# Cross attention of a decoder layer: context loaded turned, its norm moved into the key-value weights

## The chip, the cores and the metric

The kernel runs on one core of one Trainium2 chip. A core has TensorE (matrix products, results in PSUM), VectorE, ScalarE and GpSimd for work on elements, and a queue engine (SyncE, SP) that starts transfers between DRAM and on-chip memory (SBUF). Each engine works through its own list of instructions and waits on semaphores for the others. The metric is the device time of one execution in microseconds; lower is better.

## What is computed

A decoder layer on 32 sequences of 112 tokens, width 256: a mixer with a state-space scan and its MLP, cross attention with 16 heads over a context of 375 rows, and a feed-forward layer with 8-bit rounding. The change touches the context's side of cross attention and its preparation:

```python
def layer_norm(x, g, b):
    mu = jnp.mean(x, axis=-1, keepdims=True)
    var = jnp.var(x, axis=-1, keepdims=True)
    return (x - mu) * jax.lax.rsqrt(var + EPS) * g + b
...
kv = cn @ Wkv
k, v = jnp.split(kv, 2, axis=-1)
sim = jnp.einsum('bhid,bjd->bhij', q, k) + mask[:, None, :, :]
attn = jax.nn.softmax(sim, axis=-1)
out = jnp.einsum('bhij,bjd->bhid', attn, v)
```

Here `cn` is the layer norm of the context, with gain `cln_g` and bias `cln_b`; one key head and one value head of 64 columns serve all 16 query heads. All of it is float32.

## The kernel before

Eight groups of four sequences pass through two parts. The first 613 us belong to the **mixer** (`mixer`): for group i, tiles of the input projection, a chain of factors on VectorE and GpSimd (`softplus`, `factors`, `chain`, `right`), then `scan(i)`, which multiplies in 56-row blocks (line 375), masks the result on VectorE (`causal_part`, line 791) and multiplies again (`scan_out`, line 361). `hidden` and `down` are its MLP.

The rest is **attention** (`attention`), groups of 28 steps, seven steps per sequence. In step p TensorE computes the scores of two heads' rows (line 1393), VectorE adds the mask and finds the extreme (`highest`, line 1793), ScalarE takes the exponential (line 1666), VectorE divides one step later (`divide`, line 1802), TensorE turns the probabilities two steps later (line 1400), ScalarE copies them (line 1660), and every three or four steps TensorE multiplies them with the values (line 1416). The scores of a step wait until `highest` of the step before is done.

Between these, `schedule()` puts *pieces* at fixed places `AT[p, "X"]` and `AT[p, "Y"]`, and all engines walk the same table: gate and value tiles of the gated MLP (steps 10 to 17), output tiles (1 to 8), the way back (9), the feed-forward tiles `up` (20 to 23) and `down` (25), query tiles (27). The norms of tokens, results and final output are spread over steps 20 to 22, 10 to 12 and 25 to 27 on VectorE. Each piece's PSUM bank (`seat`) is handed on by semaphores (`vacant`, `filled`, `emptied`). `START` is the order of the pieces ahead of the first group, among the last tiles of the mixer's MLP (`("mlp", n)`).

The context of the next sequence takes this path. SyncE loads it with rows on partitions into one of two buffers `cx` (line 1303). In the first three steps of a sequence VectorE runs `context_norm`: statistics; the inverse root (ten small operations, `norm_root`, last one at line 77); the normalization in place (line 1143). In steps 3 and 4 TensorE does the piece `("turned", b, k)`, three transposes of 125x128 into PSUM (line 1500), and ScalarE copies each with the gain as scale and the bias (line 1711) into `cT`. In step 5 follows `("kv", b)`, the product of `cT` with the weights `wkv` (line 1507), in step 6 `("vback", b)`, which turns the values back (line 1513). ScalarE copies the keys twice, VectorE the values once.

Of the kernel before, what the change touches and what calls it, by code (L numbers as in the profile page):

```python
# [16 lines left out]
GB = 4  # L17
# [87 lines left out]
def mixer(nc, ctx0, PS, ident, i_in, x_dram, xm_dram, w):  # L105
# [136 lines left out]
    def sync(sp):  # L242
# [16 lines left out]
        tokens_in(2)  # L259
        for i in range(NG):  # L260
# [19 lines left out]
    def tensor(pe):  # L280
# [169 lines left out]
        pe.wait_ge(s_prep.sem, 1)  # L450
        for i in range(NG):
# [210 lines left out]
    def vector(dve):  # L662
# [210 lines left out]
        dve.wait_ge(s_w2.sem, 5 * 16)  # L873
        for i in range(NG):
# [156 lines left out]
CLN = 3 * JT + 1 + RSQRT  # L1031
# [5 lines left out]
def schedule():  # L1037
# [36 lines left out]
def seat(piece):  # L1074
# [5 lines left out]
    if piece[0] in ("turned", "kv", "vback"):  # L1080
        if piece[1] != 1:
            return 2
        return piece[2] if piece[0] == "turned" else int(piece[0] == "vback")
# [62 lines left out]
def attention(nc, ctx0, PS, apart, ident, xm_dram, ctx_dram, mask_dram, out_dram, w):  # L1146

    sb = Arena(nc, ARENA_AT)
    cx = sb("x_cx", [JP, 2, JT, D])
# [15 lines left out]
    cT = sb("x_cT", [128, KD, J])  # L1165
    kT = sb("x_kT", [128, 2, J])
# [38 lines left out]
    l_cx = [count(f"x_lcx{n}", 32) for n in range(2)]  # L1205
# [88 lines left out]

    def sync(sp, mlp):
# [6 lines left out]
        def contexts(i, b):  # L1302
            sp.dma_start(cx[:, b % 2, :, :], ctx_dram[i * GB + b, :, :].rearrange("(t p) d -> p t d", p=JP)).then_inc(l_cx[b % 2].sem, 16)
# [4 lines left out]
        def group(it, first=False, last=False):  # L1308
            for p in range(STEPS):
# [18 lines left out]
                if p == 6:  # L1328
                    filled(sp, it, ("turned", 1, 1))
                    contexts(it, 3)  # L1330
                if p == 13 and not last:
                    filled(sp, it, ("turned", 2, 1))
                    contexts(it + 1, 0)
                if p == 20 and not last:
                    filled(sp, it, ("turned", 3, 1))
                    contexts(it + 1, 1)
                if p == 26 and not last:
                    filled(sp, it, ("turned", 0, 1))
                    contexts(it + 1, 2)
# [10 lines left out]
        sp.dma_start(cols[:, :], w["x_cols"]).then_inc(l_q.sem, 16)  # L1350
        contexts(0, 0)
        contexts(0, 1)
        scanned()
        sp.dma_start(wq[:, :, :], w["x_wq"]).then_inc(l_q.sem, 16)
        sp.dma_start(wkv[:, :, :], w["x_wkv"]).then_inc(l_kv.sem, 16)
# [26 lines left out]
    def tensor(pe, mlp):  # L1382
# [235 lines left out]
        for piece in START:  # L1618
# [3 lines left out]
            if piece == ("turned", 0, 0):  # L1622
                result_taken(LAST - 1)
# [462 lines left out]
```

## Time and profile before

| | us |
|---|---|
| median of three runs | 1927.63 |
| lowest and highest | 1926.17, 1927.75 |
| the profiled execution | 1927.04 |
| its span, first to last instruction | 1925.2 |

| engine | busy, us | share of the span |
|---|---|---|
| TensorE, matmuls | 1819.9 | 95% |
| TensorE, weight loads (overlap) | 1075.7 | 56% |
| VectorE | 1286.4 | 67% |
| ScalarE | 954.6 | 50% |
| GpSimd | 420.2 | 22% |

The DMA queue of SyncE occupies 15.1% of the transfer engines' time. The granted clock of TensorE was 0.982 of full speed in the mean. Busy shares are means over stages with different limits; a busy TensorE says nothing of how its matmuls overlap. The chain that ended last tells on which engine the end hung, and the rows in order of time tell what stands where.

### The profile page before, as it was taken

To read this page: it belongs to the slowest core of one execution; us is meant where nothing else is said; L and a number is where in the kernel's file an instruction comes from. 1 tells how busy PE (TensorE), PEld (TensorE's weight loads), DVE (VectorE), ACT (ScalarE), POOL (GpSimd) and SP (SyncE) were. 2 spreads that over 40 slices of the span, in tenths; PEclk is the share of its full clock that TensorE was granted. 3 is DMA by queue.
4 is the path that set the end of the run, shared out by engine and by line. 5 is a ranking of instruction groups with operands and counts; after the bars stand their busy time and mean duration, and the time that the engine had idled before them with its cause. 6 is when DMAs were issued, how large, how long until landed. Compare 5 with 4: busy or idle time off the path is not lost.

```text
span 1925.2 us, 28637 instructions
## 1 busy us (share of the span) xinstructions
PE 1819.9 (95%) x9696; PEld 1075.7 (56%) x9696; DVE 1286.4 (67%) x3998; ACT 954.6 (50%) x2326; POOL 420.2 (22%) x569
## 2 busy tenths in 40 slices
PE   4589999999999998999999999999999999999997
PEld 2456766766767544455455555555545555555566
DVE  6688888888867487376567557557747655764743
ACT  3343553553441456456455545545645654654542
POOL 4777876876871000000000000000000000000000
PEclk8689999999999999999999999999999999999998
DMA  4000000000013232111121112112111111111100
GB/s 124 1 1 11 11 10 11 20 11 14 8 36 125 56 126 61 37 54 50 45 59 48 50 50 57 46 45 54 53 50 50 49 50 55 48 50 45 37 16 20
DMA packets 63538, 84.01 MB, mean 44 GB/s; under 512 B 5121, under 2 KB 62113, under 8 KB 62497
## 3 DMA queue, kind: packets, MB, share of 16 engines
q1 hardware_dynamic: 62928, 81.72, 15.1%
q8 instruction: 79, 1.29, 0.3%
q14 instruction: 67, 0.54, 0.1%
q10 hardware_dynamic: 464, 0.46, 0.1%
HBM read 74.82 MB, written 7.34 MB: 43 GB/s over the span
## 4 chain that ended last, share of the span: by engine, by line
PE 89%; DVE 7%; ACT 2%; issue 1%; DMA 0%; DVEq 0%; ACTq 0%
PE ps L1438 19%; PE ps L1393 9%; PE ps L1431 9%; PE ps L1400 9%; PE ps L1416 8%; PE ps L292 7%; PE ps L429 5%; PE ps L411 4%; PE ps L375 4%; PE ps L391 3%; PE ps L1507 2%; PE ps L1547 1%; PE ps L1492 1%; PE ps L361 1%; PE ps L1500 1%
## 5 line engine op out<-in xcount | busy, mean ns | idle before, releaser
L1793 DVE CUSTOM_DVE_ANT_0 x_pr<-ps,x_mk 128x375 f32<-128x375 f32 x448 | 228.0, 546 | 322.5 <-issue 204.2
L1660 ACT ACTIVATE x_pT<-ps 125x384 f32<-125x384 f32 x448 | 195.6, 490 | 252.6 <-PE ps L1400 251.8
L1666 ACT ACTIVATE x_pr<-x_pr,x_mx 128x375 f32<-128x375 f32 x448 | 268.3, 608 | 38.2 <-DVE x_mx L1793 38.1
L1400 PEld LDWEIGHTS ps<-ident,x_pr 128*125 128x125 f32 x1344 | 163.8, 187 | 129.6 <-issue 96.8
L1393 PE MATMUL ps<-x_kT,x_qT 64*128 64x375 f32 x896 | 202.5, 527 | 23.3 <-DVE x_mx L1793 17.3
L1400 PE MATMUL ps<-ident,x_pr 128*125 128x128 f32 x1344 | 206.1, 290 | 0.1
L1438 PE MATMUL ps<-x_xn,x_w 128*128 128x448 f32 x512 | 203.9, 541 | 0.0
L1802 DVE TENSOR_SCALAR x_pr<-x_pr,x_rc 128x375 f32<-128x375 f32 x448 | 169.6, 421 | 8.0
L1416 PE MATMUL ps<-x_pT,x_va 125*64 125x512 f32 (+1 forms) x768 | 159.9, 552 | 0.6 <-ACT x_pT L1660 0.6
L292 PE MATMUL ps<-m_xa,w_in 128*128 128x448 f32 x352 | 145.3, 560 | 6.2 <-ACT m_xa L522 6.2
L1393 PEld LDWEIGHTS ps<-x_kT,x_qT 64*128 64x128 f32 x896 | 68.2, 184 | 143.7 <-issue 115.8
L1438 PEld LDWEIGHTS ps<-x_xn,x_w 128*128 128x128 f32 x512 | 92.8, 190 | 74.2 <-issue 71.4
L1676 ACT ACTIVATE x_OT<-ps 128x512 f32<-128x512 f32 x64 | 34.8, 544 | 188.3 <-PE ps L1416 188.3
L429 PE MATMUL ps<-fc,m_gl 128*112 128x256 f32 x512 | 113.3, 379 | 0.1
L1416 PEld LDWEIGHTS ps<-x_pT,x_va 125*64 125x64 f32 x768 | 49.7, 137 | 94.3 <-issue 93.4
L292 PEld LDWEIGHTS ps<-m_xa,w_in 128*128 128x128 f32 x352 | 66.9, 196 | 62.6 <-issue 55.7
L429 PEld LDWEIGHTS ps<-fc,m_gl 128*112 128x112 f32 x512 | 89.4, 177 | 19.6 <-issue 0.5
L1438 PE MATMUL ps<-x_xn,x_wq 128*128 128x448 f32 x256 | 99.2, 542 | 0.0
L1438 PE MATMUL ps<-f_xn,f_w 128*128 128x448 f32 x224 | 89.5, 543 | 0.0
L1431 PE MATMUL ps<-x_ff,x_w 128*128 128x448 f32 x224 | 89.5, 542 | 0.0
L1666 ACT ACTIVATION_READ_ACCUMULATOR x_pr<-x_pr,x_mx 128x1 f32 x448 | 89.3, 199 | 0.0
L1431 PE MATMUL ps<-x_OT,x_wo 128*128 128x448 f32 x224 | 88.9, 539 | 0.0
(194 smaller groups left out, 2999.1 us busy)
## 6 DMA issues: line engine op xcount, KB each, us to landing
x_mk<-in_mask SPq DMA_DIRECT2D x224, 187.5 KB, 2.4
x_cx<-in_context SPq DMA_DIRECT2D x32, 375.0 KB
x_mixed<-m_x SPq DMA_DIRECT2D x8, 448.0 KB, 3.4
X<-x_mixed SPq DMA_DIRECT2D x8, 448.0 KB, 4.5
m_X<-in_x SPq DMA_DIRECT2D x7, 448.0 KB, 4.0
out<-f_so SPq DMA_DIRECT2D x7, 448.0 KB, 3.4
fc<-in_fc SPq DMA_DIRECT2D x2, 1024.0 KB, 13.1
x_w<-in_x_w SPq DMA_DIRECT2D x1, 2048.0 KB, 8.3
```

Source lines behind the costliest of these rows:

```text
L292: last = pe.matmul(to, w_in[:, k, n * 128:(n + 1) * 128], xa[:, k, :], start=(k == 0), stop=(k == KD - 1))
L375: last = pe.matmul(bank(2 * (b % 2) + g)[0:rows, at], Rb[part, c, b, j * S:j * S + rows], Lm[part, c, b * NQ + j, :, :], start=(c == 0), s ...
L429: last = pe.matmul(bank(4 + b // 2 if i < LAST else 4)[0:S, (b % 2) * D:(b % 2 + 1) * D], gl[:, k, b * S:(b + 1) * S], fc2[:, k, :], start ...
L1393: pe.matmul(bank(e)[:, 0:J], qT[rows, b, r * ROWS:(r + 1) * ROWS], kT[rows, b % 2, :], start=True, stop=True).then_inc(h_s.sem, 1)
L1400: last = pe.transpose(bank(2 + e)[0:JP, t * ROWS:(t + 1) * ROWS], pr[:, 2 * (p % SLOT) + e, t * JP:(t + 1) * JP], ident[:, :])
L1416: last = pe.matmul(bank(4)[DH * e:DH * e + DH, 0:n * ROWS], va[:, b % 2, t, :], pT[:, k + e:k + 2 * n:2, t, :], start=(t == 0), stop=(t == ...
L1431: last = pe.matmul(to[:, 0:T], lhs, rhs, start=(m == 0), stop=(m == KA + KH - 1))
L1438: last = pe.matmul(to[:, 0:T], weights[:, k, at:at + 128], moving[:, k, :], start=(k == 0), stop=(k == KD - 1))
L1660: act.activation(pT[:, 2 * NV * (batch(p) % 2) + 2 * (p % NP % NV) + e, :, :].rearrange("p t s -> p (t s)"), bank(2 + e)[0:JP, 0:JT * ROWS ...
L1666: act.activation(pr[:, k, :], pr[:, k, :], ACT.Exp, scale=-1.0, bias=mx[:, k:k + 1], accum_out=sums[:, k:k + 1]).then_inc(h_e.sem, 1)
L1793: dve.tensor_tensor_reduce(pr[:, k + e, :], bank(e)[:, 0:J], mk[:, p % SLOT, :], -1.0, 3.0e38, ALU.add, ALU.min, mx[:, k + e:k + e + 1]).t ...
L1802: dve.tensor_scalar(pr[:, k + e, :], pr[:, k + e, :], rc[:, k + e:k + e + 1], None, ALU.mult).then_inc(h_n.sem, 1)
```

## The change

The context is given to the kernel a second time, transposed, and loaded directly as `cT`. The copy with rows on partitions is still loaded, into one buffer, for the statistics alone. The layer norm is taken apart. Gain and mean go into the weights once: `centred` multiplies row d of `wkv` by the gain and subtracts, for each column, the mean over the rows of gain times weight, so that the product with the raw context already has its mean removed. The bias times the weights becomes a column `kvb`, added when keys and values leave PSUM. The inverse root of each context row must scale a column of `cT`: the 375 roots are written to DRAM (`roots_out`), read back onto all 128 partitions as `rb` (`roots_in`), and VectorE multiplies `cT` by it (two products of 128x375, `context_norm` stage 2). This stage moves from the third to the fifth step of a sequence (`CONTEXT = (0, 1, 4)`). The pieces `turned` with their transposes and ScalarE copies are gone; `kv` and `vback` keep their steps. In `START` the first `kv` and `vback` stand later.

```diff
@@ mixer, tensor @@
         pe.wait_ge(s_prep.sem, 1)
+        pe.wait_ge(a_dB.sem, a_dB.value(0, 2))
+        column_means(pe)
         for i in range(NG):
             scan(i)
@@ mixer, vector @@
         dve.wait_ge(s_w2.sem, 5 * 16)
+        centred(dve)
         for i in range(NG):
@@ schedule @@
-    for b, places in ((1, ((3, "X"), (4, "X"), (5, "X"), (6, "X"))), (2, ((10, "X"), (11, "X"), (12, "X"), (13, "X"))),
-                      (3, ((17, "X"), (18, "X"), (19, "X"), (20, "X"))), (0, ((24, "X"), (25, "X"), (26, "X"), (27, "X")))):
-        for place, piece in zip(places, (("turned", b, 0), ("turned", b, 1), ("kv", b), ("vback", b))):
-            at[place].insert(0, piece)
+    for b in range(GB):
+        for r, kind in ((NP - 2, "kv"), (NP - 1, "vback")):
+            at[(b - 1) % GB * NP + r, "X"].insert(0, (kind, b))
@@ attention @@
+    def early_loads(sp):
+        sp.dma_start(cols[:, :], w["x_cols"]).then_inc(l_kv.sem, 16)
+        sp.dma_start(wkv[:, :, :], w["x_wkv"]).then_inc(l_kv.sem, 16)
+
+    def column_means(pe):
+        pe.wait_ge(w_col.sem, 1)
+        for k in range(KD):
+            pe.matmul(bank(4)[:, 0:2 * DH], cgm[:, k:k + 1].to_broadcast([128, 128]), wkv[:, k, :], start=(k == 0), stop=(k == KD - 1))
+        for k in range(KD):
+            last = pe.matmul(bank(4)[:, 2 * DH:2 * DH + 1], wkv[:, k, :], cb[:, k:k + 1], start=(k == 0), stop=(k == KD - 1))
+        last.then_inc(w_mean.sem, 1)
+        pe.wait_ge(w_done.sem, KD + 1)
+
+    def centred(dve):
+        dve.wait_ge(l_kv.sem, 2 * 16)
+        dve.tensor_scalar(cgm[:, :], cg, 1.0 / D, None, ALU.mult).then_inc(w_col.sem, 1)
+        dve.wait_ge(w_mean.sem, 1)
+        for k in range(KD):
+            dve.scalar_tensor_tensor(out=wkv[:, k, :], in0=wkv[:, k, :], scalar=cg[:, k:k + 1], in1=bank(4)[:, 0:2 * DH],
+                                     op0=ALU.mult, op1=ALU.subtract).then_inc(w_done.sem, 1)
+        dve.tensor_copy(kvb[:, :], bank(4)[:, 2 * DH:2 * DH + 1]).then_inc(w_done.sem, 1)
@@ attention, sync @@
+        def turned_in(i, b):
+            sp.dma_start(cT[:, :, :], ctx_turned[i * GB + b, :, :].rearrange("(k p) j -> p k j", p=128)).then_inc(l_ct.sem, 16)
+
+        def roots_out(i, b):
+            sp.wait_ge(c_ln.sem, c_ln.value(i, CLN * b + CROOT))
+            sp.dma_start(roots_dram[:, :], st[0:JP, 16 + JT:16 + 2 * JT]).then_inc(l_rs.sem, 16)
+
+        def roots_in(i, b):
+            sp.wait_ge(l_rs.sem, l_rs.value(i, 16 * (b + 1)))
+            sp.dma_start(rb[:, :], roots_dram[:, :].rearrange("p t -> (p t)").unsqueeze(0).to_broadcast([128, J])).then_inc(l_rb.sem, 16)
...
+                if r == 1:
+                    filled(sp, made_in(it, b), ("kv", b))
+                    turned_in(g, n)
+                if r == 2:
+                    roots_out(g, n)
+                    if g + (n + 1) // GB < NG:
+                        contexts(g + (n + 1) // GB, (n + 1) % GB)
+                if r == 3:
+                    roots_in(g, n)
...
         sp.dma_start(w1[:, :, :], w["x_w1"]).then_inc(l_w1.sem, 16)
+        roots_out(0, 0)
+        contexts(0, 1)
+        roots_in(0, 0)
@@ attention, tensor @@
-            elif kind == "turned":
...
-                for t in range(JT):
-                    last = pe.transpose(to[:, t * JP:(t + 1) * JP], cx[:, b % 2, t, n * 128:(n + 1) * 128], ident[0:JP, 0:JP])
-                last.then_inc(done, 1)
             elif kind == "kv":
-                for k in range(KD):
-                    emptied(pe, it, ("turned", n, k))
+                pe.wait_ge(c_ln.sem, c_ln.value(held_by(it, n), CLN * (n + 1)))
@@ attention, scalar @@
-                act.activation(cT[:, n, :], src[:, 0:J], ACT.Identity, scale=cg[:, n:n + 1], bias=cb[:, n:n + 1]).then_inc(done, 1)
...
-                act.activation(kT[0:DH, n % 2, :], src[0:DH, 0:J], ACT.Copy)
+                act.activation(kT[0:DH, n % 2, :], src[0:DH, 0:J], ACT.Identity, bias=kvb[0:DH, :])
@@ attention, vector @@
-                norm_apply(dve, lambda t: cx[:, c, t, :], lambda t: cx[:, c, t, :], c_mv[0:JP], c_st[0:JP], c_ln, JT)
+                dve.wait_ge(l_ct.sem, l_ct.value(i, 16 * (b + 1)))
+                dve.wait_ge(l_rb.sem, l_rb.value(i, 16 * (b + 1)))
+                for k in range(KD):
+                    dve.tensor_tensor(cT[:, k, :], cT[:, k, :], rb[:, :], ALU.mult).then_inc(c_ln.sem, 1)
```

TensorE's list ahead of the first scan, before (`m_xa` is the mixer's normed input, `m_Lm` and `m_R` the scan's factors; the first 56 rows are block 0):

```order
L292 MATMUL ps<-m_xa,w_in 128x448 [waits a_xn,a_abs]
L292 MATMUL ps<-m_xa,w_in 128x448
L375 MATMUL ps<-m_Lm,m_R 16x64 [waits a_Lm,a_uTc,a_R,m_prep,m_w2]
L375 MATMUL ps<-m_Lm,m_R 16x64 x3
L375 MATMUL ps<-m_Lm,m_R 32x64 x4
```

And in the changed kernel (`x_wkv` are the key-value weights, `x_cgm` the gain over 256):

```order
L293 MATMUL ps<-m_xa,w_in 128x448 [waits a_xn,a_abs]
L293 MATMUL ps<-m_xa,w_in 128x448
L1314 MATMUL ps<-x_wkv,x_cgm 128x128 [waits a_dB,w_col,m_prep,m_w2]
L1314 MATMUL ps<-x_wkv,x_cgm 128x128
L1316 MATMUL ps<-x_cols,x_wkv 128x1 x2
L376 MATMUL ps<-m_Lm,m_R 16x64 [waits a_Lm,a_R,a_uTc,w_done]
L376 MATMUL ps<-m_Lm,m_R 16x64 x3
```

The scan now waits for `w_done`, which VectorE raises; VectorE's list has the counterpart behind the cast of the causal mask:

```order
L874 CAST causal<-m_gl 112x448 [waits m_caus]
L1322 TENSOR_SCALAR x_cgm<-x_cols 128x2 [waits x_lkv,m_w2,m_zero]
L1325 SCALAR_TENSOR_TENSOR x_wkv<-x_wkv,x_cols,ps 128x128 [waits w_mean]
L1325 SCALAR_TENSOR_TENSOR x_wkv<-x_wkv,x_cols,ps 128x128
L1327 COPY x_kvb<-ps 128x1
L794 COPY_PREDICATED m_MT<-causal,ps 112x448 [waits b_mt] x4
```

Four instructions stand there ahead of the first masked copy, which used to follow the cast.

TensorE's list in step 18 of a group and into step 19, before (`x_pr` probabilities, `x_cx` context, `f_x` tokens of the feed-forward layer):

```order
L1400 MATMUL ps<-ident,x_pr 125x128 [waits h_c,h_n]
L1400 MATMUL ps<-ident,x_pr 125x128 x2
L1500 MATMUL ps<-ident,x_cx 128x125 [waits x_free2]
L1500 MATMUL ps<-ident,x_cx 128x125 x2
L1445 MATMUL ps<-ident,f_x_127 128x112 [waits x_free0,o_ln]
L1445 MATMUL ps<-ident,f_x_127 128x112 x3
```

And in the changed kernel:

```order
L1445 MATMUL ps<-ident,x_pr 125x128 [waits h_c,h_n]
L1445 MATMUL ps<-ident,x_pr 125x128 x2
L1490 MATMUL ps<-ident,f_x_130 128x112 [waits x_free0,o_ln]
L1490 MATMUL ps<-ident,f_x_130 128x112 x3
```

The three transposes are gone and the next piece follows directly; the same holds at the seven other places of a group.

VectorE's list in step 25 of a group, before (`x_th` holds the rounded sum, `f_so` the final tokens):

```order
L1799 RECIPROCAL x_rc<-x_sum 128x2 [waits h_e]
L1802 TENSOR_SCALAR x_pr<-x_pr,x_rc 128x375 [waits h_r]
L1802 TENSOR_SCALAR x_pr<-x_pr,x_rc 128x375
L1874 TENSOR_TENSOR x_th<-ps,f_b2q 112x512 [waits x_full0]
L1878 TENSOR_TENSOR f_so<-x_th,f_x_127 112x512 [waits f_out,x_free0]
```

And in the changed kernel:

```order
L1828 RECIPROCAL x_rc<-x_sum 128x2 [waits h_e]
L1831 TENSOR_SCALAR x_pr<-x_pr,x_rc 128x375 [waits h_r]
L1831 TENSOR_SCALAR x_pr<-x_pr,x_rc 128x375
L1844 TENSOR_TENSOR x_cT<-x_cT,x_rb 128x375 [waits x_lrb,x_lct]
L1844 TENSOR_TENSOR x_cT<-x_cT,x_rb 128x375
L1906 TENSOR_TENSOR x_th<-ps,f_b2q 112x512 [waits x_full0]
L1910 TENSOR_TENSOR f_so<-x_th,f_x_130 112x512 [waits f_out,x_free0]
```

The two products with the spread roots stand in front of the evacuation of the `down` product, with the waits for the two transfers.

## Rows read from the trace of the kernel before

**Rows 1.** The page, the chain that ended last, by engine.

```profile
PE 89%; DVE 7%; ACT 2%; issue 1%; DMA 0%; DVEq 0%; ACTq 0%
```

**Rows 2.** Groups by line: names, shapes, count | busy us, mean ns | idle before.

```profile
L1711 ACT ACTIVATE x_cT<-ps,x_cols 128x375 f32<-128x375 f32 x64 | 42.3, 660 | 0.0
...
L1143 DVE TENSOR_SCALAR x_cx<-x_cx,x_mv,x_st 125x256 f32<-125x256 f32 x96 | 33.7, 407 | 0.0
...
L1500 PE MATMUL ps<-ident,x_cx 125*128 125x125 f32 x192 | 31.2, 270 | 0.1
```

**Rows 3.** TensorE in order of time, a steady group: start us, duration us, instructions.

```profile
1030.63 0.48 PE L1500 MATMUL ps<-ident,x_cx 125*128 125x125 f32 x3
1030.95 3.17 PE L1438 MATMUL ps<-x_xn,x_w 128*128 128x448 f32 x8
...
1068.37 0.48 PE L1500 MATMUL ps<-ident,x_cx 125*128 125x125 f32 x3
1068.83 3.67 PE L1492 MATMUL ps<-f_w2q,f_hq 128*112 128x256 fp8e4 x32
```

**Rows 4.** The same view, step 27; in brackets the idle time before, and its releaser.

```profile
1076.54 0.90 PE L1393 MATMUL ps<-x_kT,x_qT 64*128 64x375 f32 x4 [1.09 <-DVE x_mx L1793]
```

**Rows 5.** VectorE in order of time, steps 22 and 25 of the same group.

```profile
1057.83 0.16 DVE L77 SCALAR_TENSOR_TENSOR x_st<-x_st 125x3 f32<-125x3 f32 x1
...
1068.95 0.74 DVE L1802 TENSOR_SCALAR x_pr<-x_pr,x_rc 128x375 f32<-128x375 f32 x2
1070.80 0.69 DVE L1874 TENSOR_TENSOR x_th<-ps,f_b2q 112x512 f16<-112x512 f32 x1 [1.10 <-PE ps L1492]
```

**Rows 6.** VectorE in order of time, a float32 product out of SBUF.

```profile
83.74 0.62 DVE L748 TENSOR_TENSOR m_D<-m_rs,m_L 128x448 f32<-128x448 f32 x1
```

**Rows 7.** TensorE in order of time, the first scan.

```profile
78.43 7.67 PE L375 MATMUL ps<-m_Lm,m_R 64*16 64x64 f32 x112 [3.13 <-POOL m_R L987]
91.72 1.76 PE L361 MATMUL ps<-m_MT,m_uT 112*64 112x112 f32 x16 [5.63 <-DVE m_MT L791]
...
96.97 0.99 PE L361 MATMUL ps<-m_MT,m_uT 112*64 112x112 f32 x16
97.89 2.38 PE L375 MATMUL ps<-m_Lm,m_R 64*16 64x64 f32 x56
```

**Rows 8.** VectorE in order of time, the same stretch.

```profile
90.04 0.39 DVE L871 CAST causal<-m_gl 112x448 int8<-112x448 f32 x1
...
93.53 1.05 DVE L799 SCALAR_TENSOR_TENSOR m_u<-m_u,cols,ps 128x112 f32<-128x112 f32 x4 [0.78 <-PE ps L361]
```

**Rows 9.** TensorE in order of time, products with one moving column.

```profile
115.57 1.64 PE L319 MATMUL ps<-cols,m_r 128*112 128x1 f32 x16
```

**Rows 10.** Stretches: bounds us, length, TensorE busy (count), granted clock, DMA share, GB/s.

```profile
95.00:96.00 1.00, 1.00 (x20) 0.50 0.00 0
...
97.00:98.00 1.00, 1.00 (x22) 1.00 0.00 0
```

**Rows 11.** The page, transfers: issues, KB each, median us to landing.

```profile
x_mk<-in_mask SPq DMA_DIRECT2D x224, 187.5 KB, 2.4
...
x_w<-in_x_w SPq DMA_DIRECT2D x1, 2048.0 KB, 8.3
```

**Rows 12.** Stretches, all engines: a microsecond in which only contexts are loaded.

```profile
559.00:560.00 1.00, 1.00 (x7) 0.81 (x6) 0.96 (x3) 0.91 (x2) 1.00 (x1) 1.00 0.34 121
```

**Rows 13.** The opening of attention in order of time: SyncE, VectorE, TensorE.

```profile
613.51 0.35 SPq L1363 DMA_DIRECT2D x_w<-in_x_w  x1
...
614.86 0.16 DVE L77 SCALAR_TENSOR_TENSOR x_st<-x_st 125x3 f32<-125x3 f32 x1
...
614.66 3.27 PE L481 MATMUL ps<-m_xb,fc 128*128 128x448 f32 x8 [0.48 <-ACT m_xb L593]
...
619.28 1.67 PE L481 MATMUL ps<-m_xb,fc 128*128 128x448 f32 x4
620.78 1.67 PE L1438 MATMUL ps<-x_xn,x_wq 128*128 128x448 f32 x4
```

More of the change, by code:

```diff
@@ L659, in scalar, with vector @@
         return gelu
-    def vector(dve):
+    def vector(dve, centred):
         def roots(i):
@@ L1030 @@
 RESULT, TOKENS, FINAL = (10, 11, 12), (20, 21, 22), (25, 26, 27)
-CLN = 3 * JT + 1 + RSQRT
+CONTEXT = (0, 1, 4)
+CROOT = 2 * JT + 1 + RSQRT
+CLN = CROOT + KD
 GH = GB // 2
@@ L1079, in seat @@
         return 2
[L1080 to L1083, printed above, removed]
+    if piece[0] in ("kv", "vback"):
+        return 2 if piece[1] != 1 else int(piece[0] == "vback")
     return piece[-1] % 2
@@ L1204, in attention @@
     s_q = count("f_q", 0)
-    l_cx = [count(f"x_lcx{n}", 32) for n in range(2)]
+    l_cx = count("x_lcx", 16 * GB)
+    l_ct = count("x_lct", 16 * GB)
+    l_rs = count("x_lrs", 16 * GB)
+    l_rb = count("x_lrb", 16 * GB)
+    w_col = count("w_col", 0)
+    w_mean = count("w_mean", 0)
+    w_done = count("w_done", 0)
     l_mk = [count(f"x_lmk{n}", 16 * STEPS // SLOT) for n in range(SLOT)]
@@ L1327, in group @@
                         sp.dma_start(dst, src).then_inc(l_up.sem, 16)
[L1328 to L1339, printed above, removed]
+                b, r = divmod(p, NP)
+                if last and b == GB - 1:
+                    continue
+                n, g = (b + 1) % GB, it + (b + 1) // GB
+                if r == 1:
[7 more added lines that the diff above has]
+                    roots_in(g, n)
             if not first:
@@ L1621, in tensor @@
                 continue
-            if piece == ("turned", 0, 0):
+            if piece == ("kv", 0):
                 result_taken(LAST - 1)
-            if piece == ("kv", 0):
-                pe.wait_ge(l_kv.sem, 16)
             part(-1, piece)
@@ L1705, in part @@
                 act.activation(hq[:, n, :], src[:, 0:T], ACT.Relu, bias=fb1[:, n:n + 1], saturate=False).then_inc(done, 1)
-            elif kind == "turned":
-                b = piece[1]
-                src, done = filled(act, it, piece)
-                if n == 0 and it >= 0:
-                    filled(act, it if b != 1 else it - 1, ("kv", (b - 1) % GB))
-                act.activation(cT[:, n, :], src[:, 0:J], ACT.Identity, scale=cg[:, n:n + 1], bias=cb[:, n:n + 1]).then_inc(done, 1)
             elif kind == "kv":
@@ L1919, in group @@
                 b, r = divmod(p, NP)
-                if r < 3 and not (last and b == GB - 1):
-                    context_norm(it, (b + 1) % GB, r)
+                if r in CONTEXT and not (last and b == GB - 1):
+                    context_norm(it, (b + 1) % GB, CONTEXT.index(r))
                 if p in TOKENS and not last:
@@ L1987, in program @@
         mix = mixer(nc, ctx, PS, ident, i_in, x, xm, w)
-        att = attention(nc, ctx, PS, apart, ident, xm, ctx_dram, mask_dram, out, w)
+        att = attention(nc, ctx, PS, apart, ident, xm, ctx_dram, ctx_turned, roots, mask_dram, out, w)
         block = ctx.enter_context(nc.Block())
@@ L2079 @@
     x = given("x", np.asarray(inputs["x"]))
-    context = given("context", np.asarray(inputs["ctx_1024"]))
+    context = np.asarray(inputs["ctx_1024"])
+    turned = given("context_turned", context.transpose(0, 2, 1))
+    context = given("context", context)
     mask = np.asarray(inputs["mask_BxSxS2_ff0"])
@@ L2083 @@
     out = nc.dram_tensor("out", (B, S, D), FP32, kind="ExternalOutput").ap()
-    program(nc, x, context, mask, w, out)
+    program(nc, x, context, turned, mask, w, out)
     return run_bass_kernel_spmd(nc, [arrays], core_ids=[0]).results[0]["out"]
```

61 lines of the change are left out of this document (30 added, 31 removed).

## The prediction

> **What bounds the kernel now.** I read the chain that ended last first. TensorE holds 89% of it, VectorE 7% [rows 1]. So work taken from TensorE is time, wherever TensorE has no wait behind it; work taken from ScalarE or VectorE alone is not. Then I read the rows by line for the three parts of the old path: 192 context transposes on TensorE, 64 ScalarE copies that also apply scale and bias, 96 VectorE normalizations [rows 2]. Then TensorE's order of time in a steady group of attention: rows follow each other without a gap, the context pieces among them [rows 3]. The exception in such a group is one wait of 1.09 us on VectorE [rows 4]. Last I read the start, where the change puts new work ahead of the first scan, and the transfers.
>
> **What one context piece is worth.** The row by line says 31.2 us busy for 192 transposes, 0.27 us each [rows 2], but they overlap, so busy time is the wrong price. The right one is the shift of the next row: a piece of three starts at 1030.63 and the next matmul at 1030.95, that is 0.32 us; the piece ahead of the 8-bit matmuls starts at 1068.37 and they start at 1068.83, 0.46 us [rows 3]. There are 64 pieces (32 contexts by two). Six of them, at step 25 of groups 1 to 6, have the 8-bit product behind them: 6 x 0.46 = 2.8 us. The other 58 x 0.325 = 18.8 us. Together **21.6 us** if every piece lies on the path.
>
> Do they? Two places need a look. At steps 24 and 25 TensorE would come 0.33 + 0.46 = 0.79 us earlier to the down product, and the VectorE scaling of the turned context now sits in step 25 in front of that product's evacuation. Before, VectorE finished its division at 1069.69 and then waited 1.10 us for TensorE until 1070.80 [rows 5]. The nearest row for the new operation is the float32 SBUF product of 448 columns, 0.62 us [rows 6]; two of 375 columns take 2 x 0.62 x 375/448 = 1.04 us, 1.1 with their overhead. So VectorE, 0.33 us earlier after the shorter step 24, is free at about 1070.4, and TensorE's product is ready at 1070.0. The 0.4 us lost there sits ahead of a second wait for TensorE and is gone by step 26. The scores' wait of 1.09 us [rows 4] moves along as a whole. A quarter of the saving could be lost here, not more.
>
> By the Trainium skill, "VectorE: DVE Perf Modes", the TRN2 errata section, a float32 tensor_tensor takes (N + 151)/0.96 ns, an estimate of 0.55 us for 375 columns and 1.1 us for two. For 448 columns the formula gives 0.62 us, and the trace agrees with 0.62 us [rows 6]; by it the sum would not change.
>
> The other place is steps 17 to 19, with little TensorE work in two of them. ScalarE loses two copies of 0.66 us there [rows 2], more than TensorE loses, and VectorE's three normalizations (3 x 0.41 = 1.2 us of rows, 1.05 overlapped) are replaced by 1.1 us. Neither engine gets more work, so I keep the whole saving. In group 0 VectorE is late in several steps and some of the 8 pieces (2.6 us) may be lost; I leave them in, because the old wait on the ScalarE copy of the context vanishes as well. Bounds of the gain: 21.6 + 1.5 = 23 above; 21.6 less group 0 (2.6) less the pieces of steps 24 and 25 (6 x 0.79 = 4.7) = 14.3 below.
>
> **The prologue.** The weights are now centred between the first tiles and the first scan: VectorE scales a column, TensorE multiplies, VectorE corrects the weights, and TensorE waits for it. This looks like nothing, four small matmuls. But TensorE did the first two blocks of the scan, 112 rows of matmuls from 78.43 us on, while VectorE was still busy until 90.43 with the next group's factors, and stood ready at 91.72 [rows 7, 8]. Those blocks were hidden. Now they stand behind VectorE's first free moment. Step by step: the cast ends at 90.43 [rows 8]; the column scale is a tiny operation of 0.16 us [rows 5]: 90.65. TensorE's four matmuls are 8 rows; a row of one column with 128 loaded rows takes 1.64/16 = 0.10 us at the full clock [rows 9], 0.2 at half, and the granted clock is half there, 0.50, that is 1.2 GHz [rows 10]: 1.7 us, 92.4. VectorE's two corrections cost 1.05/4 = 0.26 us each [rows 8], the bias copy 0.17: 93.1. The first block is half of 7.67 us [rows 7]: 97.0. I take the clock as full from there, as it was from 97 us on before [rows 10]; the second block is 2.38 us [rows 7]: 99.3. The first product with the weights of the scan starts there instead of at 91.72. It catches up a little, since it and the next block run at the full clock (0.99 and 2.38 overlapped, 3.3 us, where they took 96.97 - 91.72 = 5.25): 102.6 against 96.97, **5.6 us late**. From there TensorE and, in the second group, a VectorE chain fed by it run on with no slack that is not behind this point, so all of it reaches the end. Bounds: everything at full clock (92.3 + 2.4 + 2.4 + 3.3 = 100.2) costs 3.2 us; everything at half clock (93.1 + 7.7 + 5.25 = 106.1) costs 9.1 us.
>
> **The roots' round trip.** Roots go to DRAM in 125 rows of 12 bytes and come back as one row spread over 128 partitions. The trace has no such transfer. The nearest are a mask of 187.5 KB at 2.4 us and, for what can lie ahead in the queue, a context at 0.34 of the engines and 121 GB/s (384 KB, 3.2 us) [rows 11, 12]. Two in series with one context ahead: 2 x 2.4 + 3.2 = 8.0 us. The shortest time available is at the end of a group: the roots are ready at 1057.99 and VectorE wants the spread row at 1069.69 - 0.33 = 1069.4 [rows 5], 11.4 us. Everywhere else it is more, so I cost it at nothing; below that there is no gain. In the opening, roots are ready at 615.02 [rows 13], behind 2 MB of weights that land after 8.3 us [rows 11] (issued at 613.51 [rows 13], so 621.8), then 2.4, then 3.2 + 2.4: 629.8, and two products: 630.9. The first key-value product is now behind 12 tiles of 1.50 us from 614.66 on [rows 13], at 632.7. It fits with 1.8 us to spare; were it late, that is paid once. Turned contexts add 12.3 MB to a queue that is mostly idle and have three steps to land: nothing. The key-value copies get a bias, on ScalarE and VectorE, off the path: nothing.
>
> **Sum.** 21.6 - 5.6 = 16.0 us. The profiled execution took 1927.04 us (span 1925.2); the median of the runs shown is 1927.63, so the median after is 1927.63 - 16.0 = **1911.6 us**.
>
> **Rivals.**
> - *The prologue costs nothing* (VectorE or GpSimd decides the second group anyway): 1927.63 - 21.6 = 1906 us. Against it: all of VectorE's work in that stretch starts from TensorE's results. 12%.
> - *The short steps are bound elsewhere.* VectorE and ScalarE carry steps 17 to 19 and 24 to 27, and the scaling moved into steps 11 and 25, beside the two other norms, becomes what ends last: gain 14.3, less 5.6: 1918.9 us. For it: the 1.09 us wait [rows 4]. 18%.
> - *Slower: the round trip lands late.* It decides from 11.4 us on, at step 25 of groups 0 to 6, and VectorE's wait there holds the next scores. Each microsecond beyond costs 7; the gain is gone at 11.4 + 16.0/7 = 13.7 us. At 15 us it costs 25: 1937 us. Against it: 8.0 us from rows. 6%. The Trainium skill, "DMA: Bandwidth & Descriptors", speaks against the change here: its specifications say that pieces under 512 bytes are read, modified and written. No row here shows such a write. Its section on the anatomy of one DMA gives 2.0 us fixed, an estimate of 4.0 us for two, and by that nothing is late.
> - *Slower: the transposes were not on the path*, TensorE waiting as much as it saves: only the prologue stays, 1933 us. The gapless rows [rows 3] speak against it. 4%.
> - The forecast: 60%.
>
> **Range.** 1906 takes in the first rival and the upper gain (23 less 3.2 is 1907.8); 1922 takes in the lower gain with a dearer prologue (14.3 - 9.1 = 5.2 is 1922.4). About 0.2% (3.9 us) is what a measurement of this kernel can tell from no change: faster by more 0.89, within it 0.03, slower by more 0.08.
>
> **What would show it.** No context transposes; a matmul of the next piece right behind the probability transposes in steps 3, 4, 10, 11, 17, 18, 24 and 25; a steady group shorter by 2.7 us. The first product of the scan starts at about 99 us, and everything in the second group is 5 to 6 us late. VectorE's products on the context wait for no transfer. I am wrong if the groups shrink by less than 2 us, if VectorE waits for the spread roots, or if the lateness of the start fades by the fourth group.

## The result, and the profile after

The changed kernel takes **1915.5 us** (median of 4 runs, 1913.4 to 1916.9) against 1927.7 us for the kernel before (4 runs, 1926.2 to 1928.2) on the same chip: a ratio of 0.9941, 95% interval 0.9929 to 0.9952. In a later set of runs it was 1915.0 against 1927.2, 0.9933 (0.9917 to 0.9949). The gain is 12.2 us where 16.0 were forecast. The direction was right and the time lies inside the range; one term of the sum was too small by 3.8 us.

| | before | after |
|---|---|---|
| span of the profiled execution, us | 1925.2 | 1911.6 |
| VectorE's CAST, where the new prologue begins, us | 90.04 | 88.33 |
| TensorE's first token transposes of attention, us | 613.25 | 620.99 |
| from there to the end of the span, us | 1311.95 | 1290.6 |
| steady group of attention, us | 157.2 | 154.7 |

The two halves of the sum can be read apart. Attention is 21.3 us shorter; everything ahead of it is 7.7 us longer, and that in spite of an early part that ran 1.7 us faster by chance (VectorE's CAST, the conversion of the causal mask, comes 1.7 us sooner; TensorE's token transposes at 70 us fell in a stretch at half clock before, 1.70 us, and not after, 0.93). Profiles of one code differ by as much: in a second one of the changed kernel the CAST comes at 89.19 us, and in a version below that is the same up to there (the one with a longer round trip) at 90.04. From the CAST to the first token of attention it is 523.2 us before and 532.7 after (532.6 in the second profile): the prologue costs 9.5 us.

The chain that ended last, from the page of the changed kernel, answers [rows 1]; TensorE holds a little more of it:

```profile
PE 90%; DVE 6%; ACT 1%; issue 1%; DMA 1%; SPq 0%; DVEq 0%; ACTq 0%
```

TensorE's order of time in the changed kernel (start us, duration us, instructions, in brackets the idle time before and its releaser), the first scan, answers [rows 7]:

```profile
89.07 1.20 PE L1314 MATMUL ps<-x_wkv,x_cgm 128*128 128x128 f32 x4 [15.49 <-DVE x_cgm L1322]
90.06 0.85 PE L1316 MATMUL ps<-x_cols,x_wkv 128*128 128x1 f32 x4
91.68 8.27 PE L376 MATMUL ps<-m_Lm,m_R 64*16 64x64 f32 x112 [0.77 <-DVE x_kvb L1327]
99.88 1.76 PE L362 MATMUL ps<-m_MT,m_uT 112*64 112x112 f32 x16
101.57 3.23 PE L376 MATMUL ps<-m_Lm,m_R 64*16 64x64 f32 x56
104.72 0.99 PE L362 MATMUL ps<-m_MT,m_uT 112*64 112x112 f32 x16
```

VectorE in the same stretch, answers [rows 8]:

```profile
88.33 0.39 DVE L874 CAST causal<-m_gl 112x448 int8<-112x448 f32 x1
88.75 0.18 DVE L1322 TENSOR_SCALAR x_cgm<-x_cols 128x2 f32<-128x2 f32 x1
90.95 0.60 DVE L1325 SCALAR_TENSOR_TENSOR x_wkv<-x_wkv,x_cols,ps 128x128 f32<-128x128 f32 x2 [2.02 <-PE ps L1316]
91.47 0.15 DVE L1327 COPY x_kvb<-ps 128x1 f32<-128x1 f32 x1
```

The stretches of [rows 10] (bounds, length, TensorE busy, granted clock, DMA share, GB/s), now:

```profile
96.00:97.00 1.00, 1.00 (x22) 0.50 0.00 0
102.00:103.00 1.00, 1.00 (x22) 0.50 0.00 0
103.00:104.00 1.00, 1.00 (x24) 0.75 0.00 0
104.00:105.00 1.00, 1.00 (x24) 1.00 0.00 0
```

TensorE had stood idle for 15.49 us. The clock was at half (1.2 GHz) when it began again at 89.07 us and stayed there until 103 us, through the means, the two scan blocks and the first products behind them. All six profiles in which the prologue stands here show this: the clock is back 14 to 15 us after TensorE begins again. The 112 products of the two blocks take 8.27 us, all of it now on the path.

In attention the pieces are gone and the rows close up. TensorE around steps 24 to 27 of a steady group, the place of [rows 3, 4]:

```profile
1065.90 0.92 PE L1445 MATMUL ps<-ident,x_pr 128*125 128x128 f32 x6
1066.88 3.67 PE L1537 MATMUL ps<-f_w2q,f_hq 128*112 128x256 fp8e4 x32
...
1072.07 1.43 PE L1543 MATMUL ps<-x_cT,x_wkv 128*128 128x375 f32 x4
1074.58 0.90 PE L1438 MATMUL ps<-x_kT,x_qT 64*128 64x375 f32 x4 [1.08 <-DVE x_mx L1822]
```

The scores' wait for VectorE is 1.08 us, as it was (1.09). And the group's length, from its first query product to the next group's (the same row of before stood at 1081.41 and 1238.59):

```profile
1079.46 1.77 PE L1483 MATMUL ps<-x_xn,x_wq 128*128 128x448 f32 x4
...
1234.14 2.15 PE L1483 MATMUL ps<-x_xn,x_wq 128*128 128x448 f32 x5
```

154.7 us against 157.2: 2.5 us a group, where the text forecast 2.7.

The roots' way at the end of the same kind of group (SyncE's queue and VectorE): written at 1056.62, read back from 1059.67, needed at 1067.88, no wait.

```profile
1056.62 0.28 SPq L1344 DMA_DIRECT2D context_roots<-x_st  x1
1056.94 0.34 SPq L1337 DMA_DIRECT2D x_cx<-in_context  x1
1058.97 0.35 SPq L1334 DMA_DIRECT2D x_mk<-in_mask  x1
1059.67 0.35 SPq L1348 DMA_DIRECT2D x_rb<-context_roots  x1
...
1067.88 1.00 DVE L1844 TENSOR_TENSOR x_cT<-x_cT,x_rb 128x375 f32<-128x375 f32 x2
```

The row by line of the scaling shows all its waits for a transfer in the whole kernel, 6.4 us in two places: 5.4 us in the opening, under which TensorE goes on, and 1.0 us at the end of the first group.

```profile
L1844 DVE TENSOR_TENSOR x_cT<-x_cT,x_rb 128x375 f32<-128x375 f32 x64 | 32.1, 543 | 6.4 <-DMA x_rb<-context_roots 6.4
```

### The profile page after: what moved, and what is told of

Read it like the earlier page. It is cut to its first block, busy times and chain, and to the rows that moved or that the text cites. A ratio compares the mean times of both kernels' runs of the same rounds, so it can differ in the third digit from the quotient of the medians.

```text
span 1911.6 us, 28245 instructions
## 1 busy us (share of the span) xinstructions
PE 1800.1 (94%) x9512; PEld 1056.6 (55%) x9512; DVE 1285.3 (67%) x3970; ACT 925.4 (48%) x2262; POOL 418.2 (22%) x569
## 4 chain that ended last, share of the span: by engine, by line
PE 90%; DVE 6%; ACT 1%; issue 1%; DMA 1%; SPq 0%; DVEq 0%; ACTq 0%
PE ps L1483 20%; PE ps L1438 9%; PE ps L1445 9%; PE ps L1476 9%; PE ps L1461 8%; PE ps L293 7%; PE ps L430 6%; PE ps L412 4%; PE ps L376 4%; PE ps L392 3%; PE ps L1543 2%; PE ps L1583 1%; PE ps L1537 1%; PE ps L362 1%; PE ps L1549 1%
## 5 line engine op out<-in xcount | busy, mean ns | idle before, releaser
L1438 PE MATMUL ps<-x_kT,x_qT 64*128 64x375 f32 x896 | 202.5, 527 | 23.7 <-DVE x_mx L1822 17.7
L430 PE MATMUL ps<-fc,m_gl 128*112 128x256 f32 x512 | 113.2, 379 | 0.0
L430 PEld LDWEIGHTS ps<-fc,m_gl 128*112 128x112 f32 x512 | 89.4, 177 | 19.3 <-issue 0.5
## 6 DMA issues: line engine op xcount, KB each, us to landing
x_mk<-in_mask SPq DMA_DIRECT2D x224, 187.5 KB, 2.4
x_rb<-context_roots SPq DMA_DIRECT2D x32, 187.5 KB, 5.2
```

The source lines that it names most:

```text
L430: last = pe.matmul(bank(4 + b // 2 if i < LAST else 4)[0:S, (b % 2) * D:(b % 2 + 1) * D], gl[:, k, b * S:(b + 1) * S], fc2[:, k, :], start ...
L1438: pe.matmul(bank(e)[:, 0:J], qT[rows, b, r * ROWS:(r + 1) * ROWS], kT[rows, b % 2, :], start=True, stop=True).then_inc(h_s.sem, 1)
```

## Experiments

Two theories stood at the start. **A**: the prologue costs 9.5 us, because the two scan blocks have lost their cover and because TensorE, woken at half clock, stays there. **B**: the prologue costs the 5.6 us of the prediction, and the rest of the shortfall lies in attention. The comparisons name the kernel before; each set of runs had its own runs of it, all between 1925.9 and 1927.2 us in the median. A difference between two kernels of different sets is uncertain by as much as these differ, 1 to 2 us.

### The means behind the two blocks

```diff
-        column_means(pe)
         for i in range(NG):
             scan(i)
...
+                if i == 0 and b == 1:
+                    column_means(pe)
                 if b >= 1:
                     scan_out(b - 1)
```

> TensorE computes the column means after the scan's first two blocks of the first group (L376, 112 products) and ahead of the first scan_out, no longer ahead of the blocks; VectorE's part stays behind the CAST. Theory A (order): the changed kernel's prologue costs some 9.5 us, and most of it is that the 8.27 us of the two blocks, which before ran beside VectorE's softplus chain (78.43 to 86.1 us), now run behind the centring. Then the blocks go back beside the softplus, and what stays on the path is VectorE's L1322, the means on TensorE (2.0 us) and VectorE's L1325 and L1327 (0.75 us), some 3 us together, of which the clock may take a part: 1915.5 - 9.5 + 3 = 1909, the first MT product at about 93 to 94 us after the CAST's time of 88.3 and the second group's anchor (L293, 177.98) near 171.5. Theory B (the prologue costs the 5.6 us of the prediction, of which 1.6 were the blocks behind their wait, and the rest of the shortfall lies in attention): 1915.5 - 2.6 = 1913.

Measured: 1907.9 us (1907.3 to 1908.0), ratio to before 0.9900 (0.9885 to 0.9915). TensorE's rows:

```profile
78.70 7.33 PE L376 MATMUL ps<-m_Lm,m_R 64*16 64x64 f32 x112 [3.72 <-POOL m_R L992]
90.37 1.22 PE L1315 MATMUL ps<-x_wkv,x_cgm 128*128 128x128 f32 x4 [4.35 <-DVE x_cgm L1323]
91.39 0.85 PE L1317 MATMUL ps<-x_cols,x_wkv 128*128 128x1 f32 x4
94.16 1.76 PE L362 MATMUL ps<-m_MT,m_uT 112*64 112x112 f32 x16 [1.92 <-issue]
```

The blocks are back beside VectorE's softplus chain, and one moved call gives back 7.6 us. B allowed 2.6. It falls here.

### All of the prologue where the engines are idle

```diff
         rest_of_tiles(0)
+        pe.wait_ge(a_dB.sem, a_dB.value(0, 2))
+        column_means(pe)
         turn_u(0)
...
-        pe.wait_ge(a_dB.sem, a_dB.value(0, 2))
-        column_means(pe)
+        means_taken(pe)
         for i in range(NG):
             scan(i)
...
+            if i == 0:
+                mean_column(dve)
             scale_bc(i)
...
         tiles(0)
+        centred(dve)
         softplus(1)
...
         dve.wait_ge(s_w2.sem, 5 * 16)
-        centred(dve)
```

`mean_column` is the first operation of the old `centred`, `means_taken` the last wait of the old `column_means`.

> The same work in the idle time that both engines have earlier: VectorE's L1322 ahead of its wait for the first group's spread roots (3.58 us at L771), TensorE's means ahead of turn_u of group 0 (idle 11.6 us there), VectorE's L1325 and L1327 behind the first group's u (idle 8.67 us there). Theory A: the whole 9.5 us come back: 1906.0, with L346 to L293 of group 0 as in the kernel before and the first attention token at about 613.3 us instead of 620.99. Theory B: 5.6 us come back: 1909.9, with the first attention token near 615.4 us. If the new place collides with something (its bank, the clock), the token comes later than that.

Measured: 1904.9 us (1903.7 to 1906.4), ratio 0.9885 (0.9871 to 0.9900). TensorE, and behind it VectorE:

```profile
54.48 0.61 PE L1321 MATMUL ps<-x_wkv,x_cgm 128*128 128x128 f32 x4
54.92 0.51 PE L1323 MATMUL ps<-x_cols,x_wkv 128*128 128x1 f32 x4
66.97 3.74 PE L348 MATMUL ps<-ident,m_u 128*112 128x128 f32 x16 [11.54 <-DVE m_u L726]
```

```profile
66.84 0.59 DVE L1336 SCALAR_TENSOR_TENSOR x_wkv<-x_wkv,x_cols,ps 128x128 f32<-128x128 f32 x2
67.36 0.14 DVE L1338 COPY x_kvb<-ps 128x1 f32<-128x1 f32 x1
77.94 0.62 DVE L748 TENSOR_SCALAR m_rs<-ps 128x448 f32<-128x448 f32 x1 [10.44 <-ACT ps L540]
```

The same eight matmul rows take 1.0 us here, at the full clock, where they took 1.8 behind the 15 us of idleness, and both engines still wait behind them for others. This kernel, with the prologue in the idle time, was run once more beside the changed kernel, for a difference that rests on one set of runs:

> The changed kernel as it is, beside the two versions below on the same chip, so that their differences rest on the same runs: 1915.5.

> The kernel of hidden_prologue again. 10.6 us under the changed kernel if the prologue's price of the first runs holds (1904.9 against 1915.5, from different calls); 5.6 us under it by the prediction's term.

Measured: 1915.0 (1914.5 to 1915.8) and 1904.35 us (1903.9 to 1905.0), ratios to before 0.9933 (0.9917 to 0.9949) and 0.9877 (0.9861 to 0.9893). The difference is 10.6 us. In the profiles, from the transposes of the first u (L346 there, L348 here) to attention's first token, it is 554.5 against 544.7 us: 9.8.

### No prologue at all

```diff
-        column_means(pe)
...
-        centred(dve)
+    def centred(dve):
+        dve.memset(kvb[:, :], 0.0).then_inc(w_done.sem, 1)
```

> Leaves out the column means and the centring (the key-value weights are used as loaded, the bias is zero), all else as in the changed kernel. It prices the prologue by what is gained without it. Theory A: 9.5 us, 1906.0. Theory B: 5.6 us, 1909.9. Beside hidden_prologue it tells what the hidden work still costs (theory A: nothing).

Measured: 1904.5 us (1904.0 to 1906.8), ratio 0.9885 (0.9871 to 0.9900), the same as with the prologue hidden (1904.9). So the work itself costs nothing in its new place, and its old place cost all of some 10 us.

### The clock kept up

```diff
+        for _ in range(17):
+            pe.matmul(bank(4)[:, 0:T], w_in[:, 0, 0:128], xa[:, 0, :], start=True, stop=True)
         column_means(pe)
```

> The changed kernel with 17 more products of 128x448 on TensorE (their result is overwritten) in its idle 15.5 us ahead of the column means, to keep the granted clock at 1.00 until then. If the half clock is a part of the prologue's cost, the means take about 1 us instead of 2.05, the 112 products of the two blocks about 4.8 us (112 at the 42 ns of the 56 that took 2.38) instead of 8.27, the first scan_out 0.99 instead of 1.76 and the third block 2.38 instead of 3.23, together 6 us: 1909.5. If the clock plays no part (only the order): 1915.5.

Measured: 1909.7 us (1906.8 to 1911.5), ratio 0.9905 (0.9889 to 0.9922). TensorE's rows, one of VectorE's, and a stretch of four microseconds:

```profile
77.65 14.71 PE L454 MATMUL ps<-m_xa,w_in 128*128 128x448 f32 x34 [2.79 <-issue]
92.20 0.61 PE L1316 MATMUL ps<-x_wkv,x_cgm 128*128 128x128 f32 x4
...
93.92 4.69 PE L376 MATMUL ps<-m_Lm,m_R 64*16 64x64 f32 x112 [0.77 <-DVE x_kvb L1329]
98.53 0.99 PE L362 MATMUL ps<-m_MT,m_uT 112*64 112x112 f32 x16
99.45 2.38 PE L376 MATMUL ps<-m_Lm,m_R 64*16 64x64 f32 x56
```

```profile
90.02 0.18 DVE L1324 TENSOR_SCALAR x_cgm<-x_cols 128x2 f32<-128x2 f32 x1
```

```profile
88.00:92.00 4.00, 4.00 (x12) 1.00 0.00 0
```

Nothing was moved, 14.7 us of useless products were added, and the kernel is 5.8 us faster. The two blocks take 4.69 us instead of 8.27, the first product 0.99 instead of 1.76, the next block 2.38 instead of 3.23. Together with the means (1.72 us instead of 2.61 from their start to that of the blocks) these rows are 6.1 us shorter. Of the 4.8 us that still lie between this and the version with no cost (1909.7 against 1904.9), 1.9 belong to the useless products themselves: the column that the means wait for is ready at 90.20, in the changed kernel the means start 0.14 us behind it, and here they start at 92.20, when the last of these products is done. So of the prologue's 10 us, 6 to 7 are the half clock, and the order alone, at full clock, costs some 3. The Trainium skill, "TensorE: Matmul & The Clock Gate", Part 1, says that the throttled state is the default and activity releases it; the trace agrees with its two levels, 0.50 and 1.00, and in the changed kernel the release came only after 14 us of work.

The two cures don't add up:

> hidden_prologue with 11 more products of 128x448 on TensorE, three in its gap between dt_tile of group 1 and the first scan blocks, eight between these blocks and the first scan_out; their result is overwritten. If they keep the granted clock at 1.00 from 70 us on, the 112 products take 4.7 us instead of 7.7 (which buys nothing, VectorE is later), the first scan_out 0.99 instead of 1.76 and the second block 2.4 instead of 3.2: 1.6 us, 1903.3. If the clock falls all the same, the eight products take 1.7 us each and the first scan_out comes up to 7 us late: up to 1910.

Measured: 1904.65 us (1904.1 to 1906.7), ratio 0.9880 (0.9863 to 0.9896), no different from 1904.35 without. The clock did what it should from 80 us on (1.00, with the blocks at 4.69 us, first product 0.99, next block 2.38), and from the CAST to attention's first token the kernel took 520.6 us instead of 522.6. But in this execution all from 66 to 78 us ran at half clock, the projection tile in it (4 products from 72.38 us on) took 3.32 us instead of 1.74, and VectorE's CAST came later. The early clock differs like that between executions of one kernel: the same tile took 3.15 us in the first profile of the idle-time version and 1.74 in the second. That is worth as much as the 2 us.

### TensorE's transposes put back

```diff
                 to, done = vacant(pe, it, piece)
+                for k in range(KD):
+                    for t in range(JT):
+                        pe.transpose(to[:, t * JP:(t + 1) * JP], ident[0:JP, :], ident[0:JP, 0:JP])
                 for k in range(KD):
                     last = pe.matmul(to[:, 0:J], wkv[:, k, :], cT[:, k, :], start=(k == 0), stop=(k == KD - 1))
```

> The changed kernel with TensorE's 6 transposes of each context put back (of the unit matrix, into the bank that the key-value product then overwrites), nothing else of the old way. If the gain in attention is TensorE's time alone, as the prediction has it (64 pieces, 21.6 us with the two of the opening, 0.325 us a steady piece), nearly all of it goes: 1915.5 + 64 x 0.325 = 1936.3. If the short steps are bound elsewhere (the prediction's 14.3 us case): 1930. If ScalarE's L1711 copies or its wait were what the steps waited for: under 1925.

Measured: 1931.7 us (1930.1 to 1932.9), ratio 1.0030 (1.0019 to 1.0042): 16.2 us slower than the changed kernel, 17 to 19 if each is set against its own runs of the kernel before; either way less than the 20.8 expected. The six transposes of a context stand together ahead of its key-value product, not in the two steps of the old kernel. The steady group grows by 1.9 us, from 154.7 to 156.6. TensorE at the end of a group shows where the rest went:

```profile
1082.31 0.81 PE L1544 MATMUL ps<-ident 125*128 125x125 f32 x6
1082.95 1.43 PE L1546 MATMUL ps<-x_cT,x_wkv 128*128 128x375 f32 x4
1084.83 0.90 PE L1438 MATMUL ps<-x_kT,x_qT 64*128 64x375 f32 x4 [0.44 <-DVE x_mx L1825]
```

The scores behind them wait 0.44 us for VectorE where they waited 1.08: two pieces of 0.32 us run in a wait that was there. The other six of a group cost 0.32 us each. The opening and first group grow by 5.2 us for ten pieces, but 1.7 of this is a fall of the clock that this profile has and the changed kernel's doesn't: the 16 products of L430 from 654.27 us on take 5.39 us at a granted clock of 0.59 and 0.55, where they take 3.71 there. The ten pieces cost 3.5 us. And the last stretch lacks a fall of the clock that cost the changed kernel's profile 1.7 us (below). So the gain is TensorE's time, as forecast, and a piece costs its 0.32 us where TensorE doesn't wait right behind it.

### The round trip left out

The roots are neither written nor read; VectorE multiplies by ones, so the rows of the context are not scaled.

> Leaves out the round trip: the roots aren't written or read back, VectorE multiplies the turned context by a row of ones that is set once. The multiplications stay where they are. If the round trip costs nothing but the two waits that the trace shows (5.42 us of VectorE's time in the opening, under which TensorE goes on, and 0.96 us in the first group, where TensorE waits 0.9 us for the key-value product's operand): 1915.5 - 0.9 = 1914.6 at most. If the 32 small reads and writes disturb more (SyncE's queue, the masks behind them): 1912 or less.

Measured: 1912.5 us (1910.7 to 1913.8), ratio 0.9932 (0.9917 to 0.9947), 2.5 to 3 us under the changed kernel, whose runs begin at 1913.4. Set against the kernel before, the ratio is no different from the changed kernel's 0.9941 and 0.9933, so the medians don't separate the two. The profiles differ by 3.0 us. Group boundaries place it: 1.0 us in the first group, 0.3 in the seventh, and 1.7 in one place near the end, where the same 16 products of L1583 take 4.88 us in the changed kernel and 3.19 here. That is the clock. The changed kernel, then the one without the round trip:

```profile
1864.00:1865.00 1.00, 1.00 (x7) 0.89 0.51 150
1865.00:1866.00 1.00, 1.00 (x4) 0.50 0.91 278
```

```profile
1863.00:1864.00 1.00, 1.00 (x8) 1.00 0.85 249
1864.00:1865.00 1.00, 1.00 (x7) 1.00 0.66 209
```

The kernel before has that fall too, at 1878 us (4.87 us for its 16 products), and of the two profiles of the idle-time version one has it and one hasn't, so I don't count it as the round trip's. Nor the 0.3 us of the seventh group: in the version without a prologue, which has the round trip, that group takes 154.75 us against 154.70 here and 155.03 in the changed kernel. What is left is 1.0 us, of which 0.9 is the one wait of TensorE. I had expected 0.9.

### The round trip made longer

One copy of the roots from DRAM to DRAM, or three, between the write and the read:

```diff
+            for n in range(1):
+                sp.wait_ge(l_rs.sem, l_rs.value(i, 16 * (2 * b + n + 1)))
+                sp.dma_start(roots_hops[n][:, :], (roots_hops[n - 1] if n else roots_dram)[:, :]).then_inc(l_rs.sem, 16)
```

> One more copy of the roots from DRAM to DRAM between the write and the read back, so that the round trip grows from some 8.6 us (3.1 to 3.6 us to the read's issue and 5.2 to its landing) by an estimated 3, to about 11.6. The shortest time that a steady context leaves is 11.3 us (901.93 to 913.20, step 24 of seven groups). The prediction's rival decides from 11.4 us: 1915.5 to 1917, with VectorE waits of up to 0.5 us in front of L1844 in each steady group, and the first group late by up to 3 us more.

Measured: 1921.4 us (1918.9 to 1924.8), ratio 0.9977 (0.9967 to 0.9986), 5.9 us slower than the changed kernel, 7 to 8 if each is set against its own runs of the kernel before. The steady groups hardly notice it: VectorE waits in three of them, 1.6 us in all, and one is 0.5 us longer. SyncE and VectorE at step 24:

```profile
910.13 0.28 SPq L1346 DMA_DIRECT2D context_roots<-x_st  x1
913.92 0.81 SPq L1351 DMA_DIRECT2D context_roots_hop<-context_roots  x1
918.17 0.35 SPq L1353 DMA_DIRECT2D x_rb<-context_roots_hop  x1
921.50 1.01 DVE L1849 TENSOR_TENSOR x_cT<-x_cT,x_rb 128x375 f32<-128x375 f32 x2
```

11.4 us, just what the place has. The loss is in the first group, 6.3 us longer, whose steps are shorter: VectorE waits 15.3 us in four places (8.6 of it in the opening), TensorE 3.7 in one, and during that wait its clock falls.

```profile
767.99 1.01 DVE L1849 TENSOR_TENSOR x_cT<-x_cT,x_rb 128x375 f32<-128x375 f32 x2 [3.70 <-DMA x_rb<-context_roots_hop]
...
769.06 2.87 PE L1548 MATMUL ps<-x_cT,x_wkv 128*128 128x375 f32 x4 [3.65 <-DVE x_cT L1849]
```

```profile
770.00:774.00 4.00, 4.00 (x10) 0.50 0.17 48
```

> Three more copies from DRAM to DRAM: a round trip of an estimated 17 to 18 us. By the prediction's rival (gain gone at 13.7 us, 21 us slower than the forecast at 15 us) the kernel is slower than before, above 1940. If VectorE's lateness in the short steps is made up by the slack of the long ones, it is less: the seven steady groups' step 24 wait 6 us each and the first group's contexts up to 9 us, 1960 at most by a plain sum of 7 x 6, and near 1930 if half of it is given back.

Measured: 2031.9 us (2029.3 to 2033.5), ratio 1.0551 (1.0535 to 1.0567): slower than before, as the rival had it, and far slower than either of its sums. A round trip of 15.5 us at step 24 (940.61 to 956.07), up to 17 elsewhere, is late in nearly every context, not in one of four: the wait of TensorE for the scaled context comes 30 times, and the granted clock's mean falls from 0.98 to 0.96. These 30 waits are 60 us of the 116 over the changed kernel; TensorE's waits for VectorE's extreme grow by another 13.5 (17.7 to 31.2). The rest, the lower clock among it, isn't placed.

```profile
PE ps L1548 <- DVE x_cT L1849: 60.2, 30, 7.8
...
DVE x_cT L1849 <- DMA x_rb<-context_roots_hop: 122.1, 31, 12.1
```

## Why the prediction came out 3.8 us short

**The worth of a piece held, with two offsets.** Forecast 21.6, measured 21.3 in the profiled pair. Steady groups gave 2.5 us, not 2.74: the piece at step 25 was priced at 0.46 us by the shift of the next row [rows 3], but 0.22 us of this belong to the 8-bit product behind it, which now starts 0.98 us behind its transposes (1065.90, 1066.88) where other products start 0.76 behind. The piece is worth 0.24, as the sum 7 x 0.325 + 0.24 = 2.5 shows. That took 1.3 us off. The first group with the opening gave 4.7 us for ten pieces, 3.25 by the forecast's price. Of the surplus, 0.3 is a wait: TensorE's 1.2 us for ScalarE's copy are gone, 0.9 for the scaled context have come. The rest lies at the first piece of each pair of the group: from one row of scores to the next the lateness shrinks there by 0.87 (from 7.08 to 6.21), 0.63, 0.73 and 0.46 us, where the second pieces give 0.33, 0.33, 0.3 and nothing. Why the first ones were dearer no run shows; with the six transposes put back in another place, ten cost 3.5. The seventh group gave 2.15 us instead of 2.5, the 0.3 that also comes and goes without the round trip. The scores' wait at step 27 moved along as a whole, as written. The rival of the short steps falls.

**The prologue is the step that failed**, and within it one sentence: "I take the clock as full from there, as it was from 97 us on before". Laid against the rows, from the CAST's end: to the end of the means and the centring 2.67 us forecast, 2.96 measured (88.72 to 91.68); the two blocks 6.2 forecast, 8.20 measured; the first product and the next block 3.3 forecast, 4.84 measured. The differences are 0.3, 2.0 and 1.5, together 3.8, and 5.6 + 3.8 = 9.4 us, what the profiles show. Most of the 0.3 lies at the eight matmul rows of the means, all priced like products with one moving column: 1.7 us were forecast from VectorE's column scale to its correction of the weights, and 2.0 measured. The order of work was read rightly, and so was the loss of cover. The clock was carried over from the same time in the old trace: it was full there at 97 us after TensorE had worked from 91.72 us on and, ahead of a pause, from 78.43 to 86.1. The change took that work away, and left TensorE 15.5 us idle. That this idleness is what cost the clock, the run with the 17 products shows; how much of the old work would have kept it is open. In the version without a prologue, whose TensorE worked from 78.47 to 86.7 us and from 90.69 on, the profiled execution is at 0.50 until 100 us as well, and its stretch from the CAST to attention takes 525.6 us, 3.0 more than with the prologue hidden. The upper bound, all at half clock, had been written down (9.1 us); it was the likelier value, and the measured 9.5 lies above it. The lower bound was added up wrong: 92.3 + 2.4 + 2.4 + 3.3 is 100.4, and it costs 3.4 us, not 3.2. The order alone, at some 3 us, lies there. The measured time, with 9.5 in place of 5.6 and 21.3 in place of 21.6, follows: 1927.6 - 21.3 + 9.5 = 1915.8.

**The round trip cost what was said, but not where.** The estimate of 8.0 us stands: 3.0 us at step 24 from the write's issue to the read's, and 5.2 us (median) from issue to landing, 8.3. The other figure that the prediction gave, 4.0 us for two transfers, is half of that. No steady context waits. "Everywhere else it is more" than 11.4 us was wrong: the first group leaves 10.4, 10.6 and, at its end, 7.9 us, and there TensorE waits 0.9 us. In the opening the estimate was 629.8 us (637.5 with the 7.7 us of lateness); VectorE was released at 634.8 and TensorE came at 640.55, so it has a margin of 4.7 us. The rival's threshold was right to a tenth for a steady group (11.4 us just fits), its slope was not: it counted one context of a group, and the other three leave only 13 to 14 us, so that beyond this all four are late.

**Lateness doesn't fade**, as forecast: 7.76 us at the second group's tiles, 7.74 at attention's first token.

The version with the prologue in the idle time beats both kernels: 1904.35 us against 1915.0 and 1927.2.

## What to carry to other kernels

Work put ahead of a waiting engine costs more than its own rows when it also delays work that used to run under the wait: look for what is hidden there, and put the new work in an idle stretch further up. When the change makes TensorE idle before a critical stretch, price that stretch at the half clock, and don't take the clock from the same time in the old trace. Before taking a shift of the next row as a step's worth, look whether the next row has a start of its own that stays.

## What the runs showed that I had not expected

- Seventeen useless products made the kernel 5.8 us faster, because the 15.5 us of idleness they filled had cost 14 us at 1.2 GHz: from 89 to 103 us, with TensorE waiting for only 0.8 us of it, the granted clock stayed at 0.50. They ended 1.9 us too late; fewer of them were not tried.
- Falls of the clock to 0.50 behind a short wait come and go between executions: one of them, 1.7 us near the end, is in ten of the 13 profiles and absent from three, and the same kernel has it in one profile (hidden_prologue, 4.88 us for the 16 products) and not in the other (hidden_again, 3.19).
- 125 pieces of 12 bytes are written to DRAM within 2.7 to 3.8 us of their issue where no other transfer holds the queue up. Reading the 1.5 KB back over 128 partitions (187.5 KB) takes 5.2 us in the median, and 3.3 in the kernel with one more copy. What goes ahead of it differs: at 1059.67 us it follows a context (1056.94) and a mask (1058.97), and the transfer engines are 76% busy from 1060 to 1063; at 918.17 us, with the copy in between, they are idle (0.00 from 918 to 919). The copy itself is not shown to matter.
